# A linear-attention and expert layer on one core: weights turned by TensorE at the start, and another order of work between two passes

## The reference

```python
mod = (silu(c) @ wmod).reshape(1, 6, 1, -1)          # wmod is 512 x 3072
sa, ca, ga, sb, cb, gb = mod[:, 0], ..., mod[:, 5]
ga = sign(ga) * max(|ga|, 0.25); gb = sign(gb) * max(|gb|, 0.25)
h = layernorm(x) * (1 + ca) + sa
q = elu(h @ Wq.T + bq) + 1; k = elu(h @ Wk.T + bk) + 1; v = h @ Wv.T + bv   # 16 heads of 32
KV = einsum('bhsd,bhsm->bhmd', k, v)                 # a sum over all 8192 rows
Z = 1 / (einsum('bhsd,bhd->bhs', q, k.sum(rows)) + 1e-6)
x = x + ga * (einsum('bhsd,bhmd,bhs->bshm', q, KV, Z) @ Wo.T + bo)
h = layernorm(x) * (1 + cb) + sb
V = h @ fWv.T + fbv                                  # routed over 8 experts of width 32, top 2
x = x + gb * (V + sum over experts of w_e * (silu(V @ W1[e].T + b1[e]) @ W2[e].T + b2[e]))
```

## Time and profile before

| what | value |
| --- | --- |
| median of the runs | 1271.62 us |
| the profiled execution's own time | 1271.91 us |
| its span, first to last instruction | 1270.2 us |
| TensorE busy | 1224.7 us, 96% |
| VectorE, ScalarE, GpSimd busy | 78%, 42%, 43% |
| mean granted clock of TensorE | 0.993 |

### The profile page before, as it was taken

How to read it: one execution, slowest core, us unless ns; L and a number is a source line. 1 busy time by engine, 2 the same in 40 slices (tenths; PEclk the granted TensorE clock), 3 DMA queues, 4 the chain that set the end, 5 groups by cost and what they waited for, 6 DMA issues and landing times.

```text
span 1270.2 us, 18483 instructions
## 1 busy us (share of the span) xinstructions
PE 1224.7 (96%) x5742; PEld 999.4 (79%) x5742; DVE 997.0 (78%) x2275; ACT 538.0 (42%) x1117; POOL 547.8 (43%) x401
## 2 busy tenths in 40 slices
PE   8999999999999999998789999999999999999998
PEld 5788878788777788885678888788887888888887
DVE  5887788888889888877578777777877777778764
ACT  2454454545445554443334343433434334343431
POOL 1434433333334433433346464554645445364531
PEclk9999999999999999999899999999999999999999
DMA  8455534444334443432322221313223131322201
GB/s 214 157 174 178 162 122 144 145 137 126 108 105 127 133 133 108 125 116 75 83 67 67 84 92 58 100 55 96 73 78 99 51 100 59 92 84 66 84 17 51
DMA packets 131681, 131.64 MB, mean 104 GB/s; under 512 B 12328, under 2 KB 86480, under 8 KB 131584
## 3 DMA queue, kind: packets, MB, share of 16 engines
q1 hardware_dynamic: 131584, 130.47, 33.8%
HBM read 80.62 MB, written 49.81 MB: 103 GB/s over the span
## 4 chain that ended last, share of the span: by engine, by line
PE 65%; DVE 11%; POOL 11%; issue 6%; ACT 4%; DMA 1%; SPq 0%; POOLq 0%; DVEq 0%; ACTq 0%
PE ps L1475 20%; PE ps L1476 20%; PE ps L1480 20%; POOL xb L679 6%; POOL rrs L718 3%; PE ps L1662 2%; POOL rstd L711 2%; DVE x L1303 2%; DVE xT_lo L1310 1%; DVE marked L1393 1%; PE ps L1568 1%; ACT xn L879 1%; DVE zk L1201 1%; DMA wm_in<-in_L_wmod_dram 1%; DVE m L1386 1%
## 5 line engine op out<-in xcount | busy, mean ns | idle before, releaser
L705 POOL TENSOR_TENSOR cn<-c,half 128x16 f32<-128x16 f32 x32 | 104.2, 3257 | 281.5 <-DVE c L1338 281.5
L667 POOL TENSOR_TENSOR xn_lo<-xn,xn_hi 128x512 fp32r<-128x512 f32 x64 | 85.5, 1337 | 278.1 <-ACT xn_hi L780 278.1
L1475 PE MATMUL ps<-g_hi,qT_hi 128*128 128x512 f32 x256 | 104.8, 410 | 4.9 <-ACT qT_hi L843 4.9
L798 ACT ACTIVATE exp_q<-qf 128x512 f32<-128x512 f32 x64 | 40.5, 632 | 156.7 <-DVE qf L1184 156.7
L1475 PE MATMUL ps<-wk_hi,xT_hi 128*128 128x512 f32 x256 | 102.0, 398 | 2.4 <-ACT xT_hi L774 2.4
L1475 PE MATMUL ps<-wq_hi,xT_hi 128*128 128x512 f32 x256 | 102.4, 400 | 0.5 <-DVE wq_lo L1006 0.5
L1475 PE MATMUL ps<-v_hi,xT_hi 128*128 128x512 f32 x256 | 102.9, 402 | 0.0
L1475 PE MATMUL ps<-k_hi,xn_hi 128*128 128x512 f32 x256 | 102.3, 400 | 0.0
L1476 PE MATMUL ps<-g_lo,qT_hi 128*128 128x512 f32 x256 | 101.8, 398 | 0.0
L1476 PE MATMUL ps<-wq_lo,xT_hi 128*128 128x512 f32 x256 | 101.4, 396 | 0.0
L1476 PE MATMUL ps<-wk_lo,xT_hi 128*128 128x512 f32 x256 | 101.3, 396 | 0.0
(11 more groups left out here) (240 smaller groups left out, 3292.5 us busy)
## 6 DMA issues: line engine op xcount, KB each, us to landing
xin<-_attn_hidden_states_dram SPq DMA_DIRECT2D x64, 256.0 KB, 3.1
q_scratch<-qf SPq DMA_DIRECT2D x64, 256.0 KB, 3.3
xin<-_attn_hidden_states_dram SPq DMA_DIRECT2D x32, 512.0 KB, 4.1
q_in<-q_scratch SPq DMA_DIRECT2D x128, 128.0 KB, 2.9
out_dram<-qf SPq DMA_DIRECT2D x64, 256.0 KB, 2.0
xn_scratch<-xn SPq DMA_DIRECT2D x62, 256.0 KB, 2.1
xq<-xn_scratch SPq DMA_DIRECT2D x248, 64.0 KB, 2.4
wm_in<-in_L_wmod_dram SPq DMA_DIRECT2D x4, 1024.0 KB, 5.6
```

Source lines behind the costliest of these rows:

```text
L667: nc.gpsimd.tensor_tensor(quarters(xn_lo[:, 1 - s, :]), natural(xn[:, 1 - s, :]), quarters(f32(xn_hi[:, 1 - s, :])), ALU.subtract).then_in ...
L705: nc.gpsimd.tensor_tensor(cn[:].rearrange("p h e -> p (h e)"), c2[:].rearrange("p h e -> p (h e)"), half[:], ALU.pow).then_inc(cn_done, 1)
L798: nc.scalar.activation(exp_q[:, 1 - s, :], zq[:, 1 - s, :], ACT.Relu, scale=-1.0).then_inc(rq_done, 1)
L1475: nc.tensor.matmul(dst, ah, bh, start=start and n == 0, stop=False)
```

## The change

What it does, by parts:

- **Start.** Wk and Wq come as one load each, in whole rows of 2 KB. TensorE turns them, 16 transposes of 128x128 each, and ScalarE copies them out of PSUM. Wq's load stands ahead of x tile 1 and bk. The modulation row sa stays four products on TensorE; ca is added up by VectorE (`mod1`, four instructions) and then one product with ones. sa and ca are turned one after the other. 10 warming products in place of 28. GpSimd's copy of tiles 0 and 1 into `xq` goes; TensorE turns `xn` itself. A second, regrouped set of modulation columns (`mod_turn4`, `sa4_col`, `ca4_col`) is made in steps 2 and 4 (`mod_columns`, eight small transposes), from copies by ScalarE.
- **First pass.** From tile 2 on VectorE's `normed` writes `xn` regrouped; the two halves then copy it plainly.
- **Between the passes.** The q products of the last two tiles come later: tile T-2 after the last but one moment product, tile T-1 between kv and g0. `ks` is made ahead of the last moment product, whose blocks are released one by one. `outer` is one instruction of 128 columns, `kvm` four small ones of 32 partitions that read PSUM (its zeros by GpSimd beforehand). `biased_x(0)` comes ahead of GpSimd's last step, `xb` gets two buffers, `biased_x(1)` and both `q_times_ks` come early. Pair 1's output products are made in step 0 of the second pass, ahead of `turn_x2`. The first output product waits for each low half of g by itself. The filling products there go.

The core of the diff (omitted are moves of buffers, new semaphores' declarations and renamings):

```diff
-WARM_UP = 28
+WARM_UP = 10
...
-            turned_load(raw_k, Wk, wk_in)
+            sp.dma_start(raw_k[:], Wk.rearrange("(r p) f -> p r f", p=P)).then_inc(wk_in, 16)
             for b in range(KB):
                 sp.dma_start(wm_in[:, :, b, :], wm[:, b, 0:2, :]).then_inc(wma_in[b], 16)
+            sp.dma_start(raw_q[:], Wq.rearrange("(r p) f -> p r f", p=P)).then_inc(wq_in, 16)
...
-                if i == T:
+                if i == T - 2:
                     sp.wait_ge(xn_done, T)
                     bx_load(0)
-                    sp.wait_ge(q_psum, T)
+                    sp.wait_ge(weights_ready, 1)
...
-            sweep_tiles(step, -2, T)
+            sweep_tiles(step, -2, T - 1)
+            q_store(T - 2, 0)
+            sp.wait_ge(xb_done, 1)
+            bx_load(1)
+            sp.wait_ge(qz_done, 2)
+            q_load(2)
+            q_store(T - 1, 1)
...
+            sweep_tiles(step, -2, T - 2)                      # GpSimd
+            pool.wait_ge(weights_ready, 1)
+            nc.gpsimd.memset(kvm[:], 0.0).then_inc(kv_cleared, 1)
+            biased_x(0)
+            step(T - 1, (T - 1) % 2)
+            pool.wait_ge(ksq_done, KB)
             q_times_ks(0)
...
+            q_times_ks(1)
+            biased_x(1)
...
+            q_exponential(T - 2, 0)                           # ScalarE
+            for b in (1, 3):
+                act.wait_ge(m_block, b + 1)
+                nc.scalar.activation(quarters(mt[b]), natural(ps[:, b, :]), ACT.Copy, ...)
+            den_plus_eps(0)
+            qT_high(0, 0)
+            qT_high(0, 1)
             for b in range(KB):
                 nc.scalar.copy(g_hi[:, b, :], bank(f"g{b}")).then_inc(prep_hi, 1)
...
-                nc.vector.tensor_scalar(xn[:, s, :], xin[:, s, :], mv[:, s, 0:1], rstd[:, s:s + 1],
+                dst, src = (xn[:, s, :], xin[:, s, :]) if i < 2 else (quarters(xn[:, s, :]), natural(xin[:, s, :]))
+                nc.vector.tensor_scalar(dst, src, mv[:, s, 0:1], rstd[:, s:s + 1],
...
+            q_biased(T - 2, 0)                                # VectorE
+            full("ks")                                        # then ks_q (4), and:
+            taken_by(nc.vector.tensor_tensor(groups(outer[:]), groups(ks_q[:]), over(bvp_col[:], ...), ALU.mult), "ks")
+            scaled_moment(0)
+            scaled_moment(2)
+            q_feature(T - 2, 0)
+            denominators(0)
+            inverses(0)
+            full("kv")                                        # then kvm (4)
+            scaled_q(0)
+            turned_q(0)
+            denominators(1)                                   # then g_lo (4)
+            qT_low(0, 0)
+            qT_low(0, 1)
+            inverses(1)
+            residual(0, 0)
+            scaled_q(1)
+            turned_q(1)
+            residual(0, 1)
+            qT_low(1, 0)
+            q_biased(T - 1, 1)
+            qT_low(1, 1)
+            residual(1, 0)
+            x2T_low(0, 0)
+            residual(1, 1)
+            q_feature(T - 1, 1)
+            denominators(2)
...
+            turn_x(0, 0)                                      # TensorE
+            pe.wait_ge(wk_in, 16)
+            for b in range(KB):
+                turn_weight(raw_k, b, K_BANK, k_psum_turned)
             pe.wait_ge(silu_done, 1)
             for b in range(KB):
                 pe.wait_ge(wma_in[b], 16)
+                last = nc.tensor.matmul(ps[:, 0, :], c_col[:, 2, b:b + 1].to_broadcast([P, P]), wm_in[:, 0, b, :], ...)
+            pe.wait_ge(mod1_done, KB)
+            nc.tensor.matmul(ps[:, 1, :], ones[:], mod1[:], start=True, stop=True).then_inc(prep_psum, 1)
+            pe.wait_ge(wq_in, 16)
+            for b in range(KB):
+                turn_weight(raw_q, b, Q_BANK, q_psum_turned)
             bias_rows("bk", k_turn)
...
+            sweep_tiles(step, 0, T - 1)
             pe.wait_ge(ks_done, T)
             sum_rows("ks", ks_acc[:])
+            moment(T - 1, 1)
...
+            q_product(T - 1, 1)                               # after kv
+            pe.wait_ge(prep_taken, TAKE["kv"] + 1)
             for b in range(KB):
                 nc.tensor.matmul(bank(f"g{b}"), kvm[:, b, :], woT[:, b, :], start=True, stop=True).then_inc(prep_psum, 1)
...
-                if live(j, J):
+                if live(j, J) and j != 1:
                     out_product(j, 1)
-                if fill_step:
-                    warm_up(3, 6)
+                if j == 0:
+                    out_product(1, 0)
+                    out_product(1, 1)
```

More of the change, by code:

```diff
@@ L729, in step_b @@
                     row_scale(j)
[L730 removed]
+                if j == 0:
+                    q_times_ks(2)
+                if live(j + 1, J) and j >= 1:
                     biased_x(j + 1)
@@ L1222, in step @@
                 prepare(i, 1)
+                if i in (2, 4):
+                    mod_columns(1 if i == 2 else 0)
                 if i == 15:
@@ L1602, in step @@
[L1602 to L1611 removed]
+                    moment(i - 1, 1 - s)
```

388 lines of the change are left out of this document (207 added, 181 removed).

## The result

The kernel after takes 1254.31 us (median of four runs, 1254.01 to 1254.41), the kernel before 1272.36 beside it (four runs, 1271.24 to 1273.31). The ratio is 0.9858 with a 95% interval of 0.9841 to 0.9875: 18.05 us faster. The profiled execution of after took 1254.41 us, its span is 1252.7 us, 17.5 less than before's 1270.2. The forecast was 1259.3, so the direction and the places were right and the gain was larger than the 12.3 us worked out.

The account below looks back on a forecast made before the run. First pass bound by TensorE's matmuls, second by a loop through GpSimd and residual, scores just longer than TensorE's work; span 1270.2 - 5 (start) + 0.5 (first pass) - 7.8 (between) = 1257.9, forecast 1259.3 us, range 1256 to 1262.5.

Parts of the forecast that it names:

- the 4 turns of tile 0 and the 16 of Wk run slow, 20 x 0.3 = 6: Start: these TensorE transposes at half clock, less half a us for a clock rise, run from 7 to 12.5 us.
- The rival in which the start stays slow: Start: ten warming products don't raise the clock, turns and bias rows run at half, no gain; 1264.3 us, chance 0.10.
- nearest row: First pass: a regrouped row reading PSUM, 0.75 us, taken as upper price of VectorE's normed, 0.54 with plain rows.
- (a, b): Between the passes: moment ends at 586.5 with 0.8 waiting; blocks scaled as they come, 0.67 exposed; kv 587.2 to 591.2.
- (c): Between the passes: the last tile's q product fills 2.8 us while VectorE makes kvm; g runs 594.0 to 597.6.
- (d): Between the passes: scaled_q and turned_q done by 595; g's low halves pace the first output product, 598 to 601.
- (e): Between the passes: pair 1's output products run 604.5 to 610.7, hiding pair 0's norm chain, ready at 609.7.
- (f): Between the passes: two turns with x2T_low between, 2.6 us; first fused product at 613.3, 8.1 us earlier.
- (g): Next step: loses 5.6 us of products, gains only 1.1 because GpSimd's and VectorE's router chain sets it; ends at 633.4.
- The races: Between the passes: VectorE's outer and scaled_q against GpSimd's q_times_ks(0) and biased_x(1); GpSimd winning both gives 1263.0, chance 0.12.
- The slower rival: Second pass: VectorE's L1361 settles at 1.96 us in place of 1.17, costing 24.5 over 31 pairs; 1284 us, chance 0.05.
- both openings near their best ends: Full clock, races won, no wait for last k sum: 7.2 at the start, 9.4 between; 1255 us, chance 0.15.

Follow-up runs that it names:

- w0: The kernel after without any warming product; 1255.11 us.
- b_between_only: The kernel after with before's start, so the new order between the passes without the new start; 1259.81 us, ratio 0.9913 to before.
- s_start_only: The kernel before with only the change's new start and regrouped first-pass rows; 1265.53 us, ratio 0.9958 to before.
- q_first: The kernel after with the last q product ahead of the last moment product instead of between kv and g; 1259.34 us, ratio 0.9910 to before.
- outs_step1: The kernel after with pair 1's output products and VectorE's residuals for it back in step 1 of the second pass; 1252.95 us, ratio 0.9868 to before.
- early: The kernel after with ScalarE's and GpSimd's pair 1 normalisation work earlier in step 1, q_times_ks(3) later, and pair 3's denominators in step 2; 1255.60 us.
- early2: The kernel early with both of VectorE's x2T_low(1, .) ahead of scores(0) in step 1; 1252.58 us, ratio 0.9845 to before.
- xb_late: The kernel after with GpSimd's biased_x(0) behind its last step of the first pass instead of ahead of it; 1252.93 us.
- w28: The kernel after with WARM_UP at 28 warming products in place of 10; 1255.99 us.
- early2_xb_late: The kernel early2 with biased_x(0) behind GpSimd's last step of the first pass, as in xb_late; 1252.03 us, ratio 0.9843 to before.

## Why the prediction was right, and where it was off

The places, the order of the landmarks and the sign were right; the size was 5.0 us short (1259.3 and 1254.31), and the forecast's own range of 1256 to 1262.5 missed the result by 1.7. By spans the forecast was 1257.9 and the profiled execution 1252.7; the 5.2 us between them are 1.8 at the start, 0.4 in the first pass, 1.95 between the passes and 1.0 in the second pass.

**Start: forecast -5, measured -6.8.** The loads were right: Wk was there when TensorE asked for it at 7.49 (forecast 7.5), the sa products waited for wmod's loads twice and ended near 14 (forecast 16.1). The step that failed is "the 4 turns of tile 0 and the 16 of Wk run slow, 20 x 0.3 = 6": the 16 took 1.97 us, 0.123 each. The pace rose within the 20 records of warming, in most other executions of this start only with tile 0's turns, but always ahead of Wk's, and the idle of 1.3 us in after did not lose it. The price of a slow turn was too high as well: in w0, without warming, the same turns took 0.23 each, so that all 20 of them slow would be 4.6 us and not 6. The 0.3 was twice a 0.15 that is itself 0.60 us over four records, and with sixteen in a row the full pace is 0.123. "Twenty records end near 5" was early too (5.57, and up to 6.36 in the others), as a window of 1 us counts the records cut by its edges: 20 slow ones took 4.64 us, 4.3 a us and not 6. 2.1 us of the sum came from this, as `ca_col` stood at 17.03 and not 19.1. It was also the side on which the bounds were drawn: -7.5 for "all at the full clock" missed by 0.7. The rival in which the start stays slow is dead: even w0, with no warming at all, has k(1) 4.9 us ahead of before's. The bias rows for bk took 3.6 us, as forecast, at the full clock; in before they ran at 0.60 and 0.80 a record behind 3.02 us of idle, and b_between_only shows how much that depends on when the clock falls: 4.83 us up to the next product in one execution and 6.08 in the other.

**First pass: forecast +0.5, measured +0.1** (s_start_only). `normed` on regrouped columns took 538 ns in the median, 539 before: the lower bound was the true one. VectorE's reading of PSUM, the "nearest row", was nearest in its access pattern and not in its cost. Its transposes in steps 2 and 4 were covered.

**Between the passes: forecast -7.8, measured -9.75** (from kv's start on, with the q product counted: 642.63 - 626.18 = 16.45, less the 6.7 by which s_start_only's kv came sooner). By its steps, in before's time, that is after's plus 6.7: (a, b) kv at 586.3 (forecast 587.2); (c) g at 593.0 (594.0), with no idle, and q_first shows that the q product hides VectorE's masks there, and more; (d) the first output product at 596.7 (598); (e) pair 1's at 604.0 (604.5); (f) the first fused product at 612.1 (613.3); (g) the second at 632.9 (633.4). So each landmark was within 1.3 us, late by about one from (a) on, and 0.6 of that one is the wait for the last sum of k, put at 0.8: TensorE waited 0.2. What (g) took off again, 0.9 us for the clock and 0.5 for waits behind GpSimd, didn't come. The clock did fall, to 0.75 over the step (after's windows), and the value product behind the 7 us of idle ran at 0.63 us a record in place of 0.39, which is some 2 us; but VectorE's `xT_lo` at 624.84 let nothing go on before 625.5 anyway, and the next pair, at clock 1.00, took 20.1 us. The step's cost was there and its cover had been overlooked.

What the steps had wrong without harm to the sum is (e): the norm chain was to be "hidden" behind pair 1's output products. outs_step1 shows that the chain is ready at 600.9 and that the products delay TensorE's turn by 2 us and the first fused product by 1.1, more than the 0.5 us by which their absence shortens step 1 (and the 1.1 us are what is left with outs_step1's turns at the slow clock, 1.12 and 1.09 us). And the reason given for (g), "set by the router's chain", was right in a stronger form than meant: early and early2 moved the fused product by up to 7.7 us, and 1.7 was left one step later.

**The races.** VectorE won both: `outer` started at 578.29 and took 0.29 us, GpSimd's `q_times_ks(0)` at 578.34; `scaled_q(0)` started at 584.94 and took 1.23, `biased_x(1)` at 585.54 took 2.88 in place of 2.41. Who won lost nothing and who came second paid: in the first race 0.05 us decided, and GpSimd's product took 2.49 us in place of 2.38. q_first shows the second race lost: there `biased_x(1)` came 0.33 us ahead, and `scaled_q(0)` took 3.15 us. The sum had VectorE win both but gave no reason for it, so that part of it was luck; the margins, 0.05 and 0.60 us, are 0.04 and 0.60 in xb_late too. A third meeting, which the forecast named only as a thing to look for, GpSimd won: `biased_x(0)` ran from 571.47, VectorE's kf of tile 63 came at 572.15 and took 2.28 us. xb_late prices it at 0.5 us. The Trainium skill, "SBUF — State Buffer", section "Who interferes with whom", has the shared ports locked for the whole of whichever instruction comes first; these rows agree.

**Second pass: forecast 0, measured -1.0.** The pairs are 20.08 us long in after (the mean distance of 28 of GpSimd's `biased_x`), 20.11 in before. They are 20.11 in s_start_only and 20.03 in b_between_only, so it belongs to the order between the passes or to what comes with it (two buffers of `xb`). With an unchanged second pass it was 20.04 in w28 and 20.07 in w0. VectorE's second residual starts 0.08 us sooner in a pair of b_between_only than in one of before, and all else in the pair keeps its distance. Why is open; it is worth 1 to 2 us. The prediction's 0.68 us of waiting a pair was 21.1 us over all 31 places; over the 28 pairs of its own window TensorE waited 16.0 us, 0.57 a pair, and the rest lay in the steps at both ends. The slower rival, a second phase at 1.96 us for L1361, didn't come: L1388, as it is now, has a median of 1168 ns beside 1174.

The errors of the sum were all on one side, so none hid another: at the start, at (a) and at (g) an upper price was taken where the cover or the clock was in doubt. The rival "both openings near their best ends", 1255, was the case that came, and it was given 0.15.

## What to carry to other kernels

When a wait on the path is taken away, ask at once what the same instruction would have waited for next, and on which engine: here `xn`, then `xT_lo`, then `aT_lo` stood a few us apart, and 7 us of idle were worth 1.7. A product that can go anywhere belongs where another engine is late twice over, and not where TensorE merely idles: the q product taken away from between kv and g cost 5 us, a lost race and a slow stretch among them, while pair 1's output products, moved into a gap of 4.7 us, gave nothing and left one of 7 us behind. Behind the same 3.54 us of idle the clock was 0.83 in one execution and 0.66 in another, so compare two kernels up to the landmark ahead of such a gap before a microsecond behind it is put down to their orders. And price a regrouped access and the clock's level from a row of the same kind, and the landmarks from the chain, with both ends kept.

## What the runs showed of the hardware that was not expected

- The clock column can read 1.00 while TensorE runs at half pace: the window from 7 to 14 us of w0 has 1.00, and the 16 turns in it took 3.67 us beside 1.97 in after. At the start of an execution the pace of like records is the better witness.
- Turns of 128x128 run at the full clock and seem to raise it as products do: in w0 nothing but 20 turns had run, and the eight records right behind them took 4.18 us, 0.6 more than the 3.60 of the same records in w28, so that at most the first two of them can have been slow.
- The same eight records after an idle of 3.02 us took 5.6 us in one execution (before) and 6.9 in another (b_between_only); and behind the same 3.54 us of idle the clock was 0.83 in one (early2) and 0.66 in the other (early2_xb_late).
- VectorE's normalisation of 128x512 with both sides regrouped took 538 ns, as with plain ones (539).
- Of instructions locked out by GpSimd even the smallest pay in full: one of 128x16 took 2.25 us in place of 0.17.
